# Gate products of a recurrence that stream each operand three times, into one real and two scratch places of a PSUM bank

## The reference

```python
def step(H, xs):
    xz, xr, xh = xs
    Z = jax.nn.sigmoid(xz + H @ Whz.T + bhz)
    R = jax.nn.sigmoid(xr + H @ Whr.T + bhr)
    H_tilda = jnp.tanh(xh + R * H @ Whh.T + bhh)
    H_new = Z * H + (1.0 - Z) * H_tilda
    Y = H_new @ Whq.T + bhq
    return (H_new, Y)
```

## Time and profile before

| What | Value |
|---|---|
| time, median of 3 runs | 651.02 us (650.6 to 651.64) |
| the profiled execution's own time | 652.1 us |
| its span, first to last instruction | 649.9 us |
| mean granted TensorE clock in the span | 0.529 |
| TensorE busy | 626.7 us, 96% of the span |
| VectorE busy | 486.9 us, 75% |
| ScalarE busy | 209.5 us, 32% |

### The profile page before, as it was taken

The page is one execution under the profiler, slowest core; times in us unless marked ns, Lnnn a source line. Parts: engine busy times, 40 slices in busy tenths (PEclk is TensorE's granted clock), DMA queues, the critical chain, the costliest instruction groups (busy, mean ns, idle before and its releaser), DMA issues.

```text
span 649.9 us, 39744 instructions
## 1 busy us (share of the span) xinstructions
PE 626.7 (96%) x16880; PEld 567.8 (87%) x16880; DVE 486.9 (75%) x4001; ACT 209.5 (32%) x1603; POOL 23.7 (4%) x20
## 2 busy tenths in 40 slices
PE   4979999999999999999999999999999999999986
PEld 3469999999999999999999999999999999999975
DVE  3877777777777777777777777777777777777775
ACT  2033333333333333333333333333333333333332
POOL 2820000000000000000000000000000000000000
PEclk9965555555555555555555555555555555555555
DMA  7000000000000000000000000000000000000000
GB/s 259 0 4 4 5 13 3 13 4 5 12 5 12 5 12 5 5 12 4 12 5 12 5 3 13 5 12 5 12 5 3 13 4 13 5 12 4 4 12 12
DMA packets 6629, 8.85 MB, mean 14 GB/s; under 512 B 818, under 2 KB 4914, under 8 KB 6452
## 3 DMA queue, kind: packets, MB, share of 16 engines
q1 hardware_dynamic: 6016, 6.04, 2.8%
q10 hardware_dynamic: 436, 0.27, 0.2%
HBM read 4.21 MB, written 2.10 MB: 10 GB/s over the span
## 4 chain that ended last, share of the span: by engine, by line
PE 92%; DVE 5%; ACT 1%; DMA 1%; issue 1%; SPq 0%; DVEq 0%
PE chunk_bank L555 52%; PE z_rec_bank L555 13%; PE chunk_bank L547 12%; PE z_bank L547 6%; PE y_bank L532 6%; PE chunk_bank L493 2%; DMA x<-x_cm 1%; DVE xs L357 1%; DVE r_hidden L448 1%; DVE r_hidden L452 1%; DVE hidden L480 1%; ACT scan_mul L311 1%; DVE r_hidden L456 0%; DVE lin L367 0%; ACT r_bank L309 0%
## 5 line engine op out<-in xcount | busy, mean ns | idle before, releaser
L555 PE MATMUL chunk_bank<-r_hidden,w_part 128*128 128x8 bf16 x6144 | 206.6, 169 | 3.2 <-DVE r_hidden L448 2.6
L555 PEld LDWEIGHTS chunk_bank<-r_hidden,w_part 128*128 128x128 bf16 x6144 | 184.8, 105 | 20.8 <-DVE r_hidden L448 2.7
L555 PEld LDWEIGHTS chunk_bank<-hidden,w_part 128*128 128x128 bf16 x3072 | 102.2, 104 | 37.2 <-DVE hidden L480 7.4
L555 PE MATMUL chunk_bank<-hidden,w_part 128*128 128x8 bf16 x3072 | 124.9, 173 | 6.2 <-DVE hidden L480 6.2
L480 DVE TENSOR_TENSOR_SCAN hidden<-scan_mul,hidden 128x24 f32<-128x24 f32 x512 | 80.8, 200 | 66.7 <-ACT hidden L314 60.3
L311 ACT ACTIVATE scan_mul<-z_pre 128x16 f32<-128x16 f32 x256 | 57.3, 224 | 199.3 <-DVE z_pre L460 199.3
L555 PE MATMUL z_rec_bank<-hidden_parts,w_part 128*128 128x24 bf16 x3072 | 121.3, 181 | 0.0
L555 PE MATMUL chunk_bank<-hidden_parts,w_part 128*128 128x8 bf16 x3072 | 119.1, 168 | 0.0
L309 ACT ACTIVATE r_bank<-chunk_bank 128x8 f32<-128x8 f32 x256 | 41.5, 162 | 206.7 <-PE chunk_bank L555 206.7
L555 PEld LDWEIGHTS z_rec_bank<-hidden_parts,w_part 128*128 128x128 bf16 x3072 | 103.1, 104 | 0.0
L555 PEld LDWEIGHTS chunk_bank<-hidden_parts,w_part 128*128 128x128 bf16 x3072 | 103.0, 104 | 0.0
(11 more groups left out here) (71 smaller groups left out, 673.2 us busy)
## 6 DMA issues: line engine op xcount, KB each, us to landing
x<-x_cm SPq DMA_DIRECT2D x4, 512.0 KB, 8.3
out_cm<-result SPq DMA_DIRECT2D x16, 128.0 KB, 2.2
w_rec<-w_rec_cm SPq DMA_DIRECT2D x1, 768.0 KB, 7.5
w_in<-w_in_cm SPq DMA_DIRECT2D x1, 768.0 KB, 9.6
w_mod<-w_mod_cm ACTq DMA_DIRECT2D x1, 256.0 KB, 2.7
w_out<-w_out_cm SPq DMA_DIRECT2D x1, 256.0 KB, 8.3
cond<-cond_cm SPq DMA_DIRECT2D x1, 8.0 KB, 2.4
bias_rows<-gate_bias ACTq DMA_DIRECT2D x1, 4.0 KB
```

Source lines behind the costliest of these rows:

```text
L555: return nc.tensor.matmul(cols, w_part[wp][:, gate, k, m * P:(m + 1) * P], moving, start=first, stop=True, skip_group_check=True)
```

## The change

The products of R and G that had 8 moving columns get 24: the same eight columns are read three times, by a pattern whose outer step is 0 and whose count is 3. The output is a pattern of three runs of eight columns that lie 128 columns apart. R's first run is its real place at column 0, and the other two are scratch at 128 and 256. G moves to column 384, and its runs are scratch at 128 and 256 and then the real place. The two products of each gate that raise done keep eight columns.

```diff
--- before.py
+++ after.py
@@ -160,12 +160,21 @@
 
         lin_bank = chunk_bank
 
+        COPIES = 3
+        GATE_AT = {R: 0, G: COPIES * BC}
+
         def pre(parity, gate, m, lo, hi):
 
             if gate == Z:
                 return z_bank[:, m * BC + lo * B:m * BC + hi * B]
-            at = 0 if gate == R else BC
+            at = GATE_AT[gate]
             return chunk_bank[parity][m][:, at + lo * B:at + hi * B]
+
+        def pre_wide(parity, gate, m, j):
+
+            first = 0 if gate == R else 1
+            return chunk_bank[parity][m][:, :].rearrange("p (c a) -> p c a", c=COPIES + 1)[
+                :, first:first + COPIES, j * B:(j + 1) * B]
 
 
         ld_cond, ld_wmod, ld_bias, ld_bq = sem("ld_cond"), sem("ld_wmod"), sem("ld_bias"), sem("ld_bq")
@@ -293,7 +302,7 @@
 
             def seed_gate(parity, gate, k):
 
-                nc.scalar.activation(chunk_bank[parity][k][:, gate * BC:(gate + 1) * BC], bias_wide[:, k, gate, :],
+                nc.scalar.activation(pre(parity, (R, G)[gate], k, 0, BLOCK), bias_wide[:, k, gate, :],
                                      ACT.Copy).then_inc(gates_seeded, 1)
 
             act.wait_ge(wide_ready, 1)
@@ -597,9 +606,14 @@
 
             def gate_products(gate, t, p, j, parts, ready, bank1_read, rest, rest2, done):
 
-                def products(m, k, w_parts, part):
+                def products(m, k, w_parts, part, wide=True):
+                    moving = parts(k, part, part + 1)
                     for wp in range(w_parts):
-                        mm = rec(pre(p, gate, m, j, j + 1), gate, m, k, wp, parts(k, part, part + 1))
+                        if wide:
+                            mm = rec(pre_wide(p, gate, m, j), gate, m, k, wp,
+                                     moving.unsqueeze(1).to_broadcast([P, COPIES, B]))
+                        else:
+                            mm = rec(pre(p, gate, m, j, j + 1), gate, m, k, wp, moving)
                     return mm
 
                 pe.wait_ge(ready[0], t + 1)
@@ -616,10 +630,10 @@
                 products(0, 0, 1, 2)
                 products(1, 0, 2, 1)
                 pe.wait_ge(rest2[1], t + 1)
-                products(0, 1, 1, 2).then_inc(done[0], 1)
+                products(0, 1, 1, 2, wide=False).then_inc(done[0], 1)
                 products(1, 1, 2, 1)
                 products(1, 0, 1, 2)
-                products(1, 1, 1, 2).then_inc(done[1], 1)
+                products(1, 1, 1, 2, wide=False).then_inc(done[1], 1)
 
             for t in range(T):
                 p, j, n = t // BLOCK % 2, t % BLOCK, t // BLOCK
```

## The result

The changed kernel takes 674.67 us (median of 4, 674.43 to 674.68) against 651.14 us before in the same comparison. The ratio is 1.0361, its 95% interval 1.0343 to 1.0379: 3.6% slower. The forecast was 659, within 646 to 661. The direction and the place were right, the size was far off.

What follows compares the result with a forecast made beforehand. A loop of latencies, not TensorE's busy time, was taken to bound the kernel. Slower reads in R's first twelve add 37 ns less 5 to spare, 32 ns a step: 651.0 + 8.2 = 659.2, rounded to 659 us, range 646 to 661.

Steps and rivals of the forecast that it cites:

- 24 columns in 30 ns: R's first twelve products: reading the eight columns three times takes 30 ns, over the 26.9 of the weight load.
- Twelve products at +3.1 ns are 37 ns: R's first twelve: extra reading time a step, 37 ns; less 5 to spare, the last R products end 32 ns later.
- the 5 ns that I took: R's twentieth product: TensorE has 0 to 10 ns to spare before it delays the step; 5 taken.
- 37 ns without any slack: Upper bound of the step's growth from R's first twelve: 37 ns, 9.5 us in all.
- a latency loop: Whole step: a loop of latencies from scan to scan, 2.37 us, with TensorE in it once for 0.38 us.
- E: Rival on wide products' output: writing three separate runs of a bank holds them up, 30 us, 681 us; chance 0.05.
- some 13 ns in R's link: R's link at 2.4 GHz without the reading limit: 13 ns a step gained (7 to 19), 3.3 us in all.
- neither of my ways: TensorE's clock: stays at 1.2 GHz or rises to 2.4 GHz, given evens.
- Rival C: Repeat read free of charge and clock rises: 651.0 - 3.3 - 0.8 = 646.9 us (645 to 649); chance 0.14.
- about 0.22: Closing eight fp32 entries: from about 0.22 to 0.112 us each at the raised clock, 0.8 us in all.
- I had it off: G's products are not on the loop; the tanh starts 0.13 us behind the sigmoid of z in ScalarE's order.
- one some 10 ns slower costs nothing: G's half before the tanh: 10 ns quicker gives nothing, some 10 ns slower costs nothing.

Runs made afterwards that it cites:

- r0_narrow: Changed kernel with R's first twelve products back to 8 columns, the other 32 wide ones kept: 649.77 us against 649.91, ratio 1.000.
- r0_packed: Changed kernel, all 44 products wide, but R's first twelve read an older state's packed word, a value every 4 bytes: 645.76 us, ratio 0.9939.
- r0_inner: Changed kernel, but R's first twelve read each value three times in a row and write in jumps of 128 columns: 645.41 us, ratio 0.9936.
- all_inner: Changed kernel, but all 44 wide products read each value three times in a row and write in jumps of 128 columns: 644.66 us, ratio 0.9906.
- write_table: Only R's first twelve wide, five read/write forms; form 0: state every 12 bytes, values thrice in a row, adjoining writes. Forms 0-4: 26.7, 40.0, 26.7, 40.0, 40.0 ns apart.
- read_table: All products 8 columns except R's first twelve, which read every 4 to 24 bytes, once to three times over; priced at 1.97, 1.93 and 1.96 ns a line.
- rg_short: Kernel before, all narrow, with eight of the first twelve products left out of both R and G: 650.50 us, ratio 0.9987.

## Why the prediction was wrong, point by point

*The step that failed is a size: the price of reading.* The forecast had "24 columns in 30 ns" and "Twelve products at +3.1 ns are 37 ns". They are 35.8 ns apart in the mean, 8.9 more than the 26.9 before. That falls on eleven gaps, since the first two stay as they were: the fourteenth product starts 99 ns later behind the first. The link grew by 94, so the slack was about the 5 ns that I took. I had the price from how much longer one product of eight columns lasted, about 10 ns for its columns, and multiplied by three. Eight values every 12 bytes are six lines, so that is 1.67 ns a line; the stream that reads without a pause shows 1.95 in the table. The 0.3 ns, times 18 lines, are 5 ns a product, and as the weight loads hide all up to 26.9, only 3 of my 30 had counted: the term nearly tripled. The upper end of my range, "37 ns without any slack", let the slack vary and not the one number that I had extrapolated threefold. Why the duration of one product showed too low a price is not shown.

*Right:* that a latency loop and not TensorE's busy time sets the step; that the change loses in R's first twelve and nowhere else; that G's and R's other products are free at 24 columns (r0_narrow); that E, the price of separate runs, which I held for unlikely, does not exist for runs of eight; that the clock is worth some 13 ns in R's link (15 measured).

*The clock* went neither of my ways: short rises, 0.574 over the span, in 37 of 255 steps, which are 26 ns shorter than the rest in the median.

*Rival C* had the right time for the kernel without the reading cost, 646.9 of 651.0, a ratio of 0.994; r0_packed and r0_inner have 0.994. But its working was wrong by more than half: I gave 2.4 GHz 13 ns a step, all in R's link, and it gives 31, more than half of it behind G. That C's time came out is luck: in r0_packed the clock was up only a part of the time, and r0_inner paid for its slow ends.

*A slip without weight:* (2.07 - 0.42)/7, for the closing entries, is 0.24 and not "about 0.22". The term it leads to, 0.8 us, is near the 0.9 by which the eight entries were shorter in all_inner.

*G is on the loop.* I had it off, since the tanh starts 0.13 us behind the sigmoid of z whatever G does. The start does stay there, as forecast, but that is the wrong end to read. The first tanh of a step, in the kernel before and in r0_inner:

```profile
631.60 0.18 ACT L314 ACTIVATE hidden<-chunk_bank 128x8 f32<-128x8 f32 x1
```

```profile
302.75 0.16 ACT L328 ACTIVATE hidden<-chunk_bank 128x8 f32<-128x8 f32 x1
```

It is shorter at the higher clock, though the clock is TensorE's. Counted from the semaphore of G's first bank, the tanh ends 208, 207 and 206 ns later in the kernel before, the changed one and r0_inner (medians), while its start lies 31, 30 and 41 ns behind that semaphore. In r0_packed, within one execution, it is 207 at either clock, and the semaphore itself comes 91 ns behind the start of the sigmoid of z at 1.2 GHz and 81 at 2.4. So the end follows G's twentieth product, even where the start is set by ScalarE's order.

The 8 ns from scan to first rest are the same, one bank on. In r0_packed the semaphore of G's second bank comes 17 ns earlier at 2.4 GHz, the second tanh ends 18 ns earlier and the second scan 19, a fixed 232 to 233 ns behind the second tanh's semaphore; its start moves only by 9.

all_inner shows the other side. In its slow steps at 1.2 GHz all of G's wide products write in jumps, the first bank comes some 200 ns later, and the tanh starts 0.32 us behind the sigmoid of z:

```profile
43.10 0.22 ACT L326 ACTIVATE scan_mul<-z_pre 128x16 f32<-128x16 f32 x1 [0.77 <-DVE z_pre L475]
43.42 0.33 ACT L329 ACTIVATE hidden<-chunk_bank 128x8 f32<-128x8 f32 x2
```

So a slower G lengthens the step as a faster one shortens it; "one some 10 ns slower costs nothing" was wrong with the rest.

*Open:* why the clock stays up in r0_inner, goes to and fro in r0_packed and falls back at once in the changed kernel, with the same columns a step. No run isolates it.

## What to carry to other kernels

Before a moving operand (the one that streams through TensorE) is repeated, look at how its values lie: at a pace set by weight loads, a read of every 12 bytes was free once and became the bound when it was repeated. Repeating each value in place, and not the row, takes the cost away if the written columns stay in runs (form 0 of write_table). A price taken from the duration of a single operation need not be that of a stream: here it was a seventh too low, and most of it lay hidden under another cost, so that the error in the forecast was threefold. And whether a unit is on a loop is better read from ends than from starts.

## What the runs showed of the hardware

- A moving operand was read at about 1.95 ns for each 16 bytes that it enters anew, where that exceeds the pace of the weight loads (read_table). The clock makes no difference: 35.8 ns apart at 1.2 and at 2.4 GHz (the changed kernel). Reading the same value three times in a row costs nothing (write_table, form 0, 26.7 ns).
- Columns written singly, with at least one left out between, take two column times each: 40.0 ns for 24 at 1.2 GHz (write_table). Runs of eight cost nothing (r0_narrow).
- A step wholly at 2.4 GHz is 31 ns shorter than one at 1.2 GHz, 2.337 for 2.368 us (r0_packed, in one execution), although 16 products fewer a step gain only some 0.7 us in all, 3 ns a step (rg_short). The gain lies behind the last products of R (15 ns) and of G (10 ns up to the scans, 8 up to the rests).
- A ScalarE instruction can end at a fixed time after the semaphore that it waits for, whatever its recorded start: the first tanh ended 205 to 208 ns behind it with starts 22 (all_inner, slow steps), 31 (before) and 41 ns (r0_inner) behind it.
